# Sixteen-head attention on one core: the two heads of a pair in two row tiles of 64 rows of TensorE

## What is computed

```python
for l in range(4):                       # l = 1 has a causal mask, l = 2 has no MLP
    h = modulate(layernorm(x), cond)     # per sequence: factor and addend from the condition
    q, k, v = h @ Wqkv + b               # 16 heads of 16
    s = q @ k.T * scale                  # 256 x 256 for each head
    p = softmax(s)                       # with the row maximum taken off
    x = x + gate * ((p @ v) @ Wo + bo)
    x = x + gate2 * (gelu(modulate(layernorm(x)) @ W1 + b1) @ W2 + b2)   # l = 2: a second modulated norm
```

## Time and profile before

| what | us |
|---|---|
| time, median of 3 runs | 1201.8 (1199.96 to 1210.7) |
| the profiled execution: its own time | 1202.65 |
| its span, first to last instruction | 1200.8 |
| PE busy / PEld busy | 1100.7 / 840.9 |
| DVE busy | 806.5 |
| ACT busy | 560.7 |
| POOL busy | 173.5 |

### The profile page before, as it was taken

How to read it: one execution, slowest core, us unless ns; L and a number is a source line. 1 busy time by engine, 2 the same in 40 slices (tenths; PEclk the granted TensorE clock), 3 DMA queues, 4 the chain that set the end, 5 groups by cost and what they waited for, 6 DMA issues and landing times.

```text
span 1200.8 us, 22222 instructions
## 1 busy us (share of the span) xinstructions
PE 1100.7 (92%) x7540; PEld 840.9 (70%) x7540; DVE 806.5 (67%) x2245; ACT 560.7 (47%) x1122; POOL 173.5 (14%) x288
## 2 busy tenths in 40 slices
PE   5799999999999999999999988888888999999996
PEld 4567777777777777777777665555555777777765
DVE  4576667666677667766577677777778666776642
ACT  4235554545643455444554434444444455554451
POOL 3010110101102211010110011111114101111010
PEclk9789999999999999999999999999999999999998
DMA  7542333123343233312333323333353133322300
GB/s 234 181 147 72 107 108 92 59 63 105 107 151 147 78 107 107 90 56 70 106 108 116 109 63 115 105 114 112 113 164 124 58 107 116 116 76 65 92 24 18
DMA packets 102714, 123.18 MB, mean 103 GB/s; under 512 B 8992, under 2 KB 96032, under 8 KB 101600
## 3 DMA queue, kind: packets, MB, share of 16 engines
q1 hardware_dynamic: 102048, 121.73, 32.6%
q10 hardware_dynamic: 576, 0.30, 0.1%
HBM read 85.16 MB, written 35.78 MB: 101 GB/s over the span
## 4 chain that ended last, share of the span: by engine, by line
PE 68%; DVE 13%; issue 6%; DMA 5%; ACT 4%; SPq 1%; ACTq 1%; DVEq 0%; POOL 0%; POOLq 0%
PE dense L1160 12%; PE dense L1091 9%; PE s_bank L1184 9%; PE o_bank L1239 8%; PE dense L1146 8%; PE st_bank L1221 6%; DMA q_stack<-max_t 4%; DVE neg_max L790 4%; PE o_bank L1120 3%; PE o_bank L1106 2%; PE o_bank L1070 2%; PE o_bank L1246 2%; PE s_bank L1194 2%; ACT xn L550 2%; DVE s_bank L785 1%
## 5 line engine op out<-in xcount | busy, mean ns | idle before, releaser
L602 ACT ACTIVATE probs<-st_bank 128x512 f32<-128x512 f32 (+1 forms) x512 | 263.8, 568 | 251.8 <-PE st_bank L1221 188.8
L790 DVE TENSOR_REDUCE neg_max<-s_bank 128x2 f32<-128x512 f32 x384 | 256.3, 684 | 70.0 <-PE s_bank L1184 66.1
L1184 PE MATMUL s_bank<-k_stack,q_stack 96*128 96x256 f32 (+1 forms) x1024 | 232.1, 318 | 18.8 <-DMA k_stack<-qk_dram 8.3
L1184 PEld LDWEIGHTS s_bank<-k_stack,q_stack 96*128 96x128 f32 x1024 | 166.1, 194 | 71.1 <-issue 24.5
L1160 PE MATMUL dense<-w_sb,hid 128*128 128x256 f32 x768 | 201.0, 380 | 0.0
L1221 PE MATMUL st_bank<-q_stack,k_stack 98*128 98x512 f32 x384 | 151.2, 467 | 7.7 <-DMA q_stack<-max_t 6.8
L443 POOL TENSOR_TENSOR veps<-mv,eps_c 128x2 f32<-128x2 f32 x65 | 12.7, 195 | 983.6 <-DVE mv L756 902.9
L1239 PE MATMUL o_bank<-probs,v_aug 128*32 128x256 f32 (+1 forms) x2048 | 132.2, 376 | 22.1 <-ACT v_aug L542 18.1
L1160 PEld LDWEIGHTS dense<-w_sb,hid 128*128 128x128 f32 x768 | 130.5, 189 | 10.6 <-issue 0.4
L1091 PE MATMUL dense<-ht,w_sb 128*128 128x256 f32 x512 | 127.4, 389 | 3.8 <-ACT ht L550 1.5
L590 ACT ACTIVATE hid<-dense,vec 128x256 f32<-128x256 f32 x192 | 80.5, 470 | 101.2 <-PE dense L1146 101.2
(11 more groups left out here) (122 smaller groups left out, 1489.9 us busy)
## 6 DMA issues: line engine op xcount, KB each, us to landing
q_stack<-qk_dram SPq DMA_DIRECT2D x192, 128.0 KB, 2.9
k_stack<-qk_dram SPq DMA_DIRECT2D x96, 256.0 KB, 4.1
par_sb<-par_dram SPq DMA_DIRECT2D x32, 512.0 KB, 5.5
qk_dram<-q_hi SPq DMA_DIRECT2D x32, 256.0 KB, 2.2
qk_dram<-q_lo SPq DMA_DIRECT2D x32, 256.0 KB, 2.2
qk_dram<-k_hi SPq DMA_DIRECT2D x32, 256.0 KB, 2.1
qk_dram<-k_lo SPq DMA_DIRECT2D x32, 256.0 KB, 2.1
w_sb<-w SPq DMA_DIRECT2D x3, 1280.0 KB, 9.2
```

Of the source, the lines that this page charges most:

```text
L602: nc.scalar.activation(probs[p % 4][:, kt, :, q0:N], src, ACT.Exp, scale=SCORE_SCALE[l]).then_inc(p_sb, 1)
L790: nc.vector.tensor_reduce(neg_max[:, qt, 2 * p:2 * p + 2], split3(bank[:]), AX.X, ALU.max, negate=True).then_inc(s_max, 1)
L1184: ins = mm(bank[:, e * N:e * N + k1], q_stack[g.par][0:KB, 2 * p + e, qt * P:(qt + 1) * P].bitcast(F32R), k_stack[g.par][0:KB, p, 0:k1].bi ...
```

## The change

- **Stacks of 64 rows.** Head e of a pair takes partitions 64e to 64e + 63. A stack's rows stand at every fourth partition (`quad:P:4`), so that one DMA fills both heads; the fourth rows are zero in `q_stack`, but for two for each head, which carry the maxima (63 and 59 of each 64). `q_stack` has 8 column blocks instead of 16. `stack` has 7 DMAs: 3 for q, 3 for k, and one that clears the row of the low maxima from a zeroed DRAM tensor, which is filled once at the start.
- **Scores in quads.** `score(g, i)` makes four matmuls: two pairs, two heads; head 0 writes `s_bank[0]` and head 1 `s_bank[1]`, each from its own 64 rows (63 are read). It waits for all earlier reductions, since both banks are written. Order and number of the reductions are as before, but a tile j is now a head of two pairs.
- **`score_t`** makes four matmuls of 64 rows and 256 columns: `st_bank[e]` holds head e with both key halves. In the causal layer it is two mask matmuls (still of 128 rows) and six of 128 columns.
- **Maxima.** `max_rows` has 4 DMAs for each half of the heads instead of 2. In MLP steps SP issues all four; in the others ACT issues two and SP two. The turned maxima of the first half go through `st_bank[0]`, not `s_bank[0]`.
- **The hand-written order** of PE and DVE is changed in both branches.

```diff
         def max_rows(eng, g, half, members=(0, 1)):
             wait(eng, max_sb, g.count(2, half + 1))
-            h0 = half * H // 2
-            for part in range(2):
-                dst = q_stack[g.par][KB + part:KB + part + 1, h0:h0 + H // 2, :]
-                src = max_t[half][part * H // 2:(part + 1) * H // 2, :]
-                eng.dma_start(dst, src).then_inc(max_ld, 16)
+            p0, n = half * PAIRS // 2, PAIRS // 2
+            for e in members:
+                for part in range(2):
+                    r0, row = (2 * part + e) * n, e * P2 + MAX_ROWS[part]
+                    eng.dma_start(q_stack[g.par][row:row + 1, p0:p0 + n, :], max_t[half][r0:r0 + n, :]).then_inc(max_ld, 16)
...
             def stack(a):
+                for stacks, parts, spilled in ((q_stack, (0, 0, 1), q_spill), (k_stack, (2, 3, 2), k_spill)):
+                    wait(sp, spilled, a.count(32, 32))
+                    for quad, part in enumerate(parts):
+                        sp.dma_start(stacks[a.par][quad:P:4], rows_of(a, part)).then_inc(stack_ld, 16)
+                sp.dma_start(q_stack[a.par][MAX_ROWS[1]:P:P2], zero_dram).then_inc(stack_ld, 16)
...
+            def score(g, *quads):
+                for i in quads:
+                    p0, qt = i // 2 * 2, i % 2
+                    wait(pe, s_max, g.count(16, 4 * i // 2))
...
                     k1 = P if CAUSAL[g.layer] and qt == 0 else N
+                    for p in (p0, p0 + 1):
+                        for e in range(2):
+                            rows = slice(e * P2, (e + 1) * P2 - 1)
+                            c0 = (p - p0) * N
+                            ins = mm(s_bank[e][:, c0:c0 + k1],
+                                     q_stack[g.par][rows, p, qt * P:(qt + 1) * P].bitcast(F32R),
+                                     k_stack[g.par][rows, p, 0:k1].bitcast(F32R), start=True, stop=True)
+                            if p > p0:
+                                ins.then_inc(s_ps, 1)
...
             def score_t(g, *pairs):
                 for p in pairs:
...
+                    for e in range(2):
+                        wait(pe, p_sb, g.count(16, 2 * p - 1 + e))
+                        if CAUSAL[g.layer]:
+                            mm(split3(st_bank[e][:])[:, :, 0:P], ident_b[:], mask_k[:], start=True, stop=False)
+                        else:
+                            mm(st_bank[e][:, 0:N], *stacks(g, p, e, 0, 0, N), start=True, stop=True)
                     if CAUSAL[g.layer]:
+                        for e in range(2):
+                            mm(st_bank[e][:, 0:P], *stacks(g, p, e, 0, 0, P), start=False, stop=False)
+                        for e in range(2):
+                            mm(st_bank[e][:, N:N + P], *stacks(g, p, e, 1, P, N), start=False, stop=True)
+                        for e in range(2):
+                            mm(st_bank[e][:, P:N], *stacks(g, p, e, 0, P, N), start=True, stop=True).then_inc(st_ps, 1)
                         continue
-                    for kt in range(T):
-                        wait(pe, p_sb, g.count(16, 2 * p + kt - 1))
-                        mm(split3(st_bank[kt][:]), *stacks(g, p, kt, 0), start=True, stop=True).then_inc(st_ps, 1)
+                    for e in range(2):
+                        mm(st_bank[e][:, N:2 * N], *stacks(g, p, e, 1, 0, N), start=True, stop=True).then_inc(st_ps, 1)
```

230 lines of the change are left out of this document (95 added, 135 removed).

## The result

The changed kernel takes **1267.0 us** (median of 4 runs, 1264.7 to 1270.2), the kernel before 1200.9 beside it: a ratio of 1.053 over all runs, 95% interval 1.049 to 1.057. It is slower, by about what was predicted (1258), but the microseconds did not arise where the sum had put them. The profiled execution took 1270.15 us, of which the span is 1268.3.

The account below looks back on a forecast made before the run. PE bounds 23 steps; in the other 9 neither engine does, but a chain of PE, DVE and ACT. 13.5 (MLP) + 22.4 (causal) + 20 (without MLP) = +56 on 1202.65, less 0.85: 1258 us, range 1195 to 1295.

Parts of the forecast that it names:

- Row tiles side by side: Scores and score_t: two row-tile matmuls run together, a group costs 0.12 us; saves 3.7 us of PE per step, 2.3 causal.
- Rival 4: Row tiles don't run side by side: nothing saved, tile changes cost on top; 1337 us, chance 0.05.
- A change of tiles has a price: Each way into or out of row tiles costs PE 0.21 us: 3.4 per MLP step, 2.5 without MLP, 4.8 causal.
- Rivals 1 and 2: Changes free: 1, waits fall away too, 1128 us, chance 0.13; 2, DVE's chain stays, 1216 us, chance 0.10.
- The MLP step: 15 steps at +0.9 us each, summed from +1.7 - 0.5 + 0.3 - 0.6; 13.5 us in all.
- the wait at S7: MLP step: score quad 7 (tiles 14, 15) waits 1 us for DVE's reduction of tile 13; `values` 1 comes +1.7 us.
- my terms (-0.5, +0.3, -0.6): MLP step: two score tiles fewer in the up part; later maxima DMAs; second half's score_t and scores savings less changes.
- rival 3: Changes cost 0.21 us but the waits are hidden, reductions coming earlier than walked; 1217 us, chance 0.14.
- The causal step: 8 steps at +2.8 us each: +2.5 from PE's own changes, 0.3 for the maxima's DMAs; 22.4 us in all.
- The step without MLP: 8 steps, +2.5 each: DVE pauses at quads +0.8, score_t 4 awaiting DMAs +2, tile 7, split, copy 0.7 + 0.4 + 0.4, overlapping.
- so it plays no part: All three kinds of step: granted clock is 1.00 (2.4 GHz), so no time was priced for it.
- Step 0: First step: bound by first loads and unchanged, 0 us.

Follow-up runs that it names:

- e6: Changed kernel plus one constant matmul in a 64-row tile ahead of each up-part group in MLP steps, 192 in all; 1338.8 us (1.114).
- e1: Changed kernel with every score and score_t matmul reading full rows, so no tile changes and none side by side; 1288.7 us (1.072).
- e7: Changed kernel with causal masks added by 64-row tiles and SP issuing half of the maxima's DMAs in step 0 too; 1258.7 us (1.049).
- e2: Changed kernel plus 38 unused matmuls of constants in PE's waits in each step without MLP and step 0; 1229.6 us (1.023).
- e12: Changed kernel plus 38 constant matmuls per step without MLP and step 0, masks in 64-row tiles, SP's half of step 0's maxima DMAs; 1224.9 us.
- e9: Changed kernel plus constants, 64-row masks, SP's DMA half in step 0; without MLP, old order of maxima and quads bank by bank; 1222.2 us.
- e11: Kernel before plus 18 matmuls of constants in each step without MLP and step 0; 1209.8 us (1.006).

## Why the prediction was right in sum and wrong in its terms

- **Row tiles side by side: right.** The two matmuls of a pair start 2 to 4 ns apart, and a group of two costs 0.12 us (in the steps without MLP, from the first `score_t` group at 869.19 to the next at 869.40 it is 0.21 at half the clock). In the MLP step of the changed kernel the quad, way in included, takes 0.34 us and the groups of `score_t` behind it 0.12:

```profile
293.90 1.56 PE L1167 MATMUL dense<-w_sb,hid 128*128 128x256 f32 x6
295.40 0.50 PE L1185 MATMUL s_bank<-k_stack,q_stack 63*128 63x256 f32 x4
295.74 0.28 PE L1220 MATMUL st_bank<-q_stack,k_stack 64*128 64x256 f32 x2
295.86 0.28 PE L1230 MATMUL st_bank<-q_stack,k_stack 64*128 64x256 f32 x2
296.07 1.56 PE L1167 MATMUL dense<-w_sb,hid 128*128 128x256 f32 x6
```

  Rival 4 is out. The Trainium skill's rule that matmuls on distinct row groups run together, some 4 ns apart (TensorE: Matmul & The Clock Gate, The mechanism), is borne out by these starts.
- **A change of tiles has a price: right, and 0.21 each was about its size.** In the rows above six plain matmuls, two groups of the quad and two of `score_t` last from 293.90 to 296.07, 2.17 us. At 0.216 for a plain matmul and 0.117 for a group they would take 1.76. So this visit costs 0.41 us. The 59 visits of this kind in the MLP steps, with two or four groups between plain matmuls, have medians of 0.396 to 0.400: **0.20 us each way**. Their starts show four pieces: 0.09 ahead of the first group, 0.11 between the first group and the second (0.223 for 0.117), 0.09 ahead of the first plain matmul behind, and 0.10 ahead of the second (0.320 for 0.216). In e6 a visit has one group, so the second piece is not there, and 0.287 is left. e1 agrees: at 0.20 the 16 changes of an MLP step take 3.2 of the 3.7 us saved, which leaves 0.5, and e1 is 0.7 us slower; at e6's 0.145 it would be 1.4. Rivals 1 and 2, which had the changes free, are out. The Trainium skill's rule that a change of mode drains TensorE (TensorEngine Tiling (Array Packing), Key Properties) names no price; that row tiles have one agrees with it.
- **The MLP step: +0.9 predicted, -0.7 measured on average, -0.2 in the step whose rows are shown** (step 6, 36.50 and 36.27 us). The array term was right: 16 x 0.20 - 3.7 = -0.5 us for -0.3. What failed is the wait at S7, which hardly came. The rows of DVE and PE from tile 10, against the earlier trace rows:

```profile
275.37 0.69 DVE L799 TENSOR_REDUCE neg_max<-s_bank 128x2 f32<-128x512 f32 x1
...
277.96 1.17 DVE L769 TENSOR_SCALAR xn<-xg,mv,rstd 128x256 f32<-128x256 f32 x2
...
280.76 0.68 DVE L799 TENSOR_REDUCE neg_max<-s_bank 128x2 f32<-128x512 f32 x1
```

```profile
281.49 0.50 PE L1185 MATMUL s_bank<-k_stack,q_stack 63*128 63x256 f32 x4 [0.16 <-DVE neg_max L799]
...
284.24 1.07 PE L1248 MATMUL o_bank<-probs,v_aug 128*32 128x256 f32 x16 [0.57 <-ACT v_aug L550]
...
293.47 0.39 PE L1220 MATMUL st_bank<-q_stack,k_stack 64*128 64x256 f32 x2 [0.19 <-DMA q_stack<-max_t]
```

  I had walked 6.9 us from the start of tile 10 to the end of tile 13; it took 280.76 + 0.6 - 275.37 = 6.0. Of the 0.9 us less, 0.6 are `second_norm`'s (1.17 us instead of 1.74); why it is faster, no run shows. So S7 waited 0.16 us and not 1, and `values` 1 came 284.24 - 270.51 = 13.7 us after the step's first quad, against 13.0 before: +0.7, not +1.7. Behind it the step is 0.9 us shorter, where my terms (-0.5, +0.3, -0.6) gave 0.8. The wait for the maxima's DMAs was right, 0.19 us for 0.3. The agreement of the rest owes something to luck, for the products behind the -0.6, 4 x 0.22 + 7 x 0.12 - 7 x 0.21, give 0.25; with that the step comes to +1.2 and the sum to 1263. In these steps rival 3, changes at 0.21 with the waits hidden, came nearest.

  The other 0.5 us of the average lie in the kernel before. Its steps 2 to 4 took 37.2, 37.6 and 37.5 us, and those of the changed kernel 36.0, 36.4 and 36.3: these three make 3.6 of the 5.2 us. In each of them PE waits for DMAs, in two of them as here, which it hardly does in the step that the prediction was read from:

```profile
138.09 0.73 PE L1221 MATMUL st_bank<-q_stack,k_stack 98*128 98x512 f32 x2 [0.80 <-DMA q_stack<-max_t]
174.20 0.50 PE L1184 MATMUL s_bank<-k_stack,q_stack 96*128 96x256 f32 x2 [0.78 <-DMA k_stack<-qk_dram]
```

  The changed kernel's steps 1 to 7 show no wait for a DMA over 0.2 us. Whether its other DMAs are the reason was not tested.
- **The causal step: +2.8 predicted, +0.7 measured on average, +1.3 where the kernel before was not held up** (37.8 us against the 36.5 of its steps 10, 11 and 15; its steps 12 to 14 took 37.0 to 37.7). The term that was too large is the price of the 23 changes, 4.8 us. By their starts the visits of this layer cost 0.24 to 0.37 us and not 0.42, so the changes come to some 3.7 us (an estimate), less 2.3 saved: +1.4. The mechanism was right: e7 takes seven changes out, makes the masks cheaper, and gains 1.2 us a step.
- **The step without MLP: +2.5 predicted, +7.2 measured.** At the full clock (e2) it is +2.6, and of that up to 0.8 may be the constants themselves. The walk of quads, T4 and tile 7 thus had about the right size; T4 did wait for `max_t` (1.40 us) and DVE did stand between quads (1.82 us of PE's waiting at quads 1 and 2). The step that failed is the sentence that the granted clock is 1.00 in all three kinds of step "so it plays no part". It read the clock of the kernel before as a property of the step. In the eight steps PE's waits make up some 75 us in the changed kernel (the groups of its table of waits for this stretch, added), in the kernel before 34. That this new idleness took the clock is shown by e2, which filled it. The largest groups of the changed kernel's table (waiting engine and line, releaser: us in total, times, longest):

```profile
PE s_bank L1185 <- DVE neg_max L799: 33.7, 23, 1.8
PE st_bank L1220 <- DMA q_stack<-max_t: 11.4, 9, 1.5
```

  The Trainium skill says (TensorE: Matmul & The Clock Gate, What's actually happening) that the halved clock is the default and that activity lifts it. The trace agrees: 0.51 behind a stretch with PE busy 1.78 of 5 us, 0.99 with those waits filled. The rule was at hand, and would have made of the waits that I had forecast a term of their own.
- **Step 0: 0 predicted, +12.7 measured.** I had costed the four DMAs of the maxima at nothing here. T4 waited 4.17 us for them against 2.35 before, quads 1 and 2 waited 1.8 us each as in the other steps without MLP, and the clock was 0.63 in the stretch from 30 to 90 us against 0.77. Filled waits (e2) gave back 5.4 us, but nothing in e12, where SP issues half of these DMAs and T4 waited 5.73. How the 12.7 divide stays open.
- What is left without MLP at the full clock, 20 us in eight steps, is not settled either. It is neither the place of the maxima nor the coupling by quads alone, for with both undone (e9) it stays, though at a clock of 0.95. The constants' own time may be a third of it (0.8 of 2.6 us a step, by e11), and the changes of tiles have not been taken out there at the full clock.
- No run beat the kernel before. By the stages, its steps without MLP and its step 0 with e7's steps 1 to 16 and 25 on would give about 1190 us (74.0 + 254.7 + 297.3 + 36.1 + 241.9 + 253.9 + 30.9 = 1188.8 of span, an estimate from two traces). That kernel needs two layouts of the stacks in one program, and it wasn't tried.

## What to carry to other kernels

A wait that a change adds to PE costs its own length and, in a stage where PE has slack, perhaps the clock of what follows: where you forecast new idle time of PE, price the work behind it at both levels before you say that the clock plays no part. Row tiles gain little when each visit holds two to four short matmuls, because every visit pays 0.40 us (0.29 with a single matmul in it): count the visits, put row-tiled work of different kinds side by side, and bring stragglers such as masks into the same mode. And where a sum of many terms comes out right, look at its stages before believing any of them.

## What the runs showed of the hardware

- Behind a stretch of 5 us with two waits of 1.4 and 1.8 us, in which PE was busy 1.78 us, the granted clock was 0.51. With the same waits filled by short matmuls it stayed at 1.00 in that part of the step, and the kernel was 37 us faster for 342 matmuls more. Two edits that each saved 16 us at the reduced clock saved 1 us together when the clock was nearly held.
- Going from full matmuls to row tiles of 64 rows and back costs 0.40 us when the visit has two groups or more (59 visits in MLP steps), and 0.287 us when it is a single matmul of bf16 constants (122 groups, 0.833 against 1.120 us).
- Causal work of 128-column matmuls goes at 0.11 to 0.13 us each with 128 rows (e1), and at 0.11 us for two in two row tiles when the first group of a visit is past (e7).
